# Attention with high and low parts: the low part of the probabilities times 65 columns of v in place of 129

## The chip, the cores and the metric

The kernel runs on one core of one Trainium2 chip. The metric is the device time of one execution in microseconds (us), the median of the runs shown. The engines are TensorE (PE in the rows, its weight loads PEld), VectorE (DVE), ScalarE (ACT), GpSimd (POOL) and the queue that issues the DMAs (SP).

## The reference

A block of a transformer on 4 sequences of 1024 tokens of width 128: attention with 16 heads of 64, then a feed-forward part of width 352 with values rounded to four-bit floats in blocks of 16. What the change touches is the attention:

```python
q = split_heads(x @ Wq.T)
k = split_heads(x @ Wk.T)
v = split_heads(x @ Wv.T)
sim = jnp.einsum('bhid,bhjd->bhij', q, k) * scale
attn = safe_softmax(sim)      # exp(s - max) / (sum + 1e-10)
out = jnp.einsum('bhij,bhjd->bhid', attn, v)
```

All of it is float32. The kernel gets near that precision on TensorE with two 16-bit parts of each number: a high part, and what is left of it as a low part.

## The kernel before

**Tiling.** The 64 pairs of sequence and head are taken two heads at a time, in 32 pairs. Rounds 0 to 33 go over them (here numbered from 0; round r computes pair r-1 while it prepares q, k and v of the next and finishes the one before). In rounds 1 to 32 the round has four units k = 0 to 3 (head k // 2, half k % 2 of the 512 queries), and each unit has eight slots s = 0 to 7, one for each block of 128 keys. The order on every engine is the order in which its own function walks rounds, units and slots; nothing reorders it, and semaphores tie the engines together.

**A slot on TensorE** (`round_` of `tensor`, L554 to L637) has, in this order:
- in odd slots `scores(s)`, two matmuls of 64 rows and 512 columns (L586) that give VectorE the scores of a later unit for its maximum;
- the transposed scores of this unit, two matmuls of 512 columns into `st` (L605, L607). They wait until the exponential of two slots before is taken (`s_ex`);
- the products of the unit before with v (L633), eight matmuls, one per key block j. The stationary operand is a 128x128 block of probabilities, the moving operand a row of `v`. In slots 0, 1, 4 and 5 the probabilities are the high part (the upper 16 bits of `probs`, read as bf16), in slots 2, 3, 6 and 7 the low part `p_low`, called **low slots** below. They add up in `ob[0]` (slots 0 to 3) or `ob[1]` (slots 4 to 7);
- jobs of the table `JOBS`, in odd slots: the projections q, k, v, the transposes, the output projection, parts of the feed-forward.

**v.** A row of `v` for a key block and a head holds, as f16, 64 columns of the high part of v, 64 of the low part and one column of ones, which gives the sum of the probabilities; one more element is not used. `VC = 2 * DH + 1` is 129, and both kinds of slot multiply by all 129 columns.

**The other engines.** ScalarE takes the exponential of each slot (L759, 128x512), reads the sums (`sums`, L727), scales the outputs (`scaled`, L773) and takes the high parts of the projections. GpSimd makes `p_low` of each slot (L449) as soon as its exponential is there, and adds the high and low outputs (`join`, L456). A unit's low parts are needed by TensorE in slot 2 of the next unit. VectorE takes the maxima (L939, one reduction of 1024 columns per odd slot; the next `scores` waits for it, since `sm` has one pair of banks), the low parts of the projections, and the rounding steps of the feed-forward (`quant`, L1085 to L1117), which are placed by hand at certain slots.

## Time and profile before

| | |
|---|---|
| median of 3 runs | 1526.01 us (1524.71 to 1526.96) |
| profiled execution, first to last instruction | 1523.5 us |
| PE busy | 1464.8 us, 96% |
| PE weight loads busy | 973.2 us, 64% |
| POOL busy | 1251.3 us, 82% |
| ACT busy | 1164.4 us, 76% |
| DVE busy | 1081.7 us, 71% |
| L633 with `probs`, 4096 matmuls of 129 columns | 317.3 us busy, 219 ns each from start to end |
| L633 with `p_low`, 4096 matmuls of 129 columns | 316.6 us busy, 219 ns each |

A matmul's 219 ns reach from its start to its end; the next one starts long before that end, so the distance of two starts, and not the mean, says what one takes on the engine. Rounds 1 to 8 have no feed-forward; the rounding of its weights stands in rounds 5, 7 and 8. From round 9 on, rounds come in turns of two (odd and even), with the feed-forward of two tiles of tokens spread over them.

### The profile page before, as it was taken

The page shows a single profiled execution, that of the slowest core. Times are in us where ns is not written, and L with a number is a line of the kernel's source. Part 1 is how long each engine was busy: PE and PEld are TensorE (multiplying, and loading weights), DVE is VectorE, ACT ScalarE, POOL GpSimd, SP SyncE. Part 2 cuts the span into 40 slices and gives each one's busy share as a digit, 9 for nine tenths or more (in the row PEclk, how much of TensorE's full clock was granted, in tenths as well). Part 3 has the DMA queues.
Part 4 walks back from the last instruction along what each step waited for, and adds up shares of the span by engine and source line. Part 5 has one row for each costly group of instructions (what it writes and reads, how often), then busy time and mean ns, then how long its engine had stood idle before and what let it go on. Part 6 is the DMA issues. An engine that isn't in the chain of part 4 may idle for free.

```text
span 1523.5 us, 35256 instructions
## 1 busy us (share of the span) xinstructions
PE 1464.8 (96%) x13828; PEld 973.2 (64%) x13828; DVE 1081.7 (71%) x1717; ACT 1164.4 (76%) x2413; POOL 1251.3 (82%) x1391
## 2 busy tenths in 40 slices
PE   4999999999999999999999999999999999999965
PEld 2566666666666666666666666666666666666644
DVE  7666676677677777676776767677776777767467
ACT  3788888877888878787787878788787878778832
POOL 5888989878888888798888879888888888888932
PEclk8999999999999999999999999999999999999977
DMA  6111111111111111111110111111011110111000
GB/s 168 43 43 43 43 40 26 32 33 43 43 43 43 26 29 40 43 43 47 37 32 22 47 43 42 47 32 37 23 46 43 43 47 23 38 31 47 2 4 14
DMA packets 46660, 59.77 MB, mean 39 GB/s; under 512 B 8672, under 2 KB 21920, under 8 KB 46496
## 3 DMA queue, kind: packets, MB, share of 16 engines
q1 hardware_dynamic: 46336, 57.26, 16.0%
q8 instruction: 111, 1.82, 0.5%
q14 instruction: 53, 0.43, 0.1%
q10 hardware_dynamic: 160, 0.26, 0.0%
HBM read 4.80 MB, written 2.10 MB: 5 GB/s over the span
## 4 chain that ended last, share of the span: by engine, by line
PE 91%; DVE 6%; POOL 1%; ACT 1%; DMA 1%; issue 1%; SPq 0%; DVEq 0%
PE ob L633 29%; PE st L605 17%; PE st L607 14%; PE sm L586 11%; PE mb L522 5%; PE mb L538 4%; PE mb L527 3%; PE mb L1240 2%; PE mb L533 2%; POOL p_low L449 1%; DVE negm L939 1%; PE mb L1251 1%; PE mb L551 1%; PE mb L1246 1%; DMA probs<-wq 0%
## 5 line engine op out<-in xcount | busy, mean ns | idle before, releaser
L449 POOL TENSOR_TENSOR p_low<-probs 128x512 f16<-128x512 f32 x1024 | 1087.4, 1074 | 208.5 <-ACT probs L759 201.7
L759 ACT ACTIVATE probs<-st,lift,exp_scale 128x512 f32<-128x512 f32 x1024 | 793.3, 775 | 189.4 <-PE st L607 169.4
L939 DVE TENSOR_REDUCE negm<-sm 128x1 f32<-128x1024 f32 x508 | 618.1, 1217 | 148.5 <-PE sm L586 148.5
L605 PE MATMUL st<-q_hl,k_hh 128*128 128x512 f16 x1024 | 394.0, 385 | 2.3 <-DMA q_hm<-m_low 2.3
L607 PE MATMUL st<-q_hm,k_l 128*128 128x512 f16 x1024 | 388.7, 380 | 0.0
L633 PEld LDWEIGHTS ob<-v,p_low 128*128 128x128 f16 x4096 | 275.1, 97 | 123.0 <-POOL p_low L449 3.3
L633 PEld LDWEIGHTS ob<-v,probs 128*128 128x128 bf16 x4096 | 276.0, 98 | 120.7 <-ACT probs L759 0.5
L633 PE MATMUL ob<-v,p_low 128*128 128x129 f16 x4096 | 316.6, 219 | 2.5 <-POOL p_low L449 2.4
L633 PE MATMUL ob<-v,probs 128*128 128x129 f16 x4096 | 317.3, 219 | 0.2
L586 PE MATMUL sm<-k_hh,q_hl 64*128 64x512 f16 x508 | 197.5, 389 | 5.7 <-DVE negm L939 5.3
L586 PE MATMUL sm<-k_hh,q_hm 64*128 64x512 f16 x508 | 197.5, 389 | 0.0
L605 PEld LDWEIGHTS st<-q_hl,k_hh 128*128 128x128 f16 x1024 | 99.1, 97 | 134.0 <-issue 116.4
L773 ACT ACTIVATE oscl<-ob,rden 128x128 f32<-128x128 f32 x512 | 157.7, 363 | 1.8 <-DVE rden L928 1.8
L456 POOL TENSOR_TENSOR o_n<-oscl 128x128 f32<-128x128 f32 x256 | 120.3, 470 | 5.4 <-ACT oscl L773 5.4
L607 PEld LDWEIGHTS st<-q_hm,k_l 128*128 128x128 f16 x1024 | 100.5, 98 | 16.3 <-issue 2.8
L907 DVE TENSOR_TENSOR v<-mb,v 128x512 f16<-128x512 f32 x64 | 44.2, 691 | 69.9 <-ACT v L696 69.9
L586 PEld LDWEIGHTS sm<-k_hh,q_hl 64*128 64x128 f16 x508 | 47.0, 93 | 62.7 <-DVE negm L939 6.5
L922 DVE TENSOR_TENSOR x<-x,mb 128x512 f32<-128x512 f32 x64 | 44.0, 687 | 54.9 <-PE mb L538 54.9
L896 DVE SCALAR_TENSOR_TENSOR k_low<-mb,k_scale,k_high 128x512 f16<-128x512 f32 x64 | 47.9, 750 | 49.2 <-ACT k_high L689 49.2
L890 DVE TENSOR_TENSOR q_low<-mb,q_high 128x512 f16<-128x512 f32 x64 | 44.2, 691 | 41.3 <-ACT q_high L682 41.3
L538 PE MATMUL mb<-wo_s,oT 128*128 128x128 f32 x512 | 70.5, 281 | 0.8 <-ACT oT L693 0.8
L696 ACT ACTIVATE v<-mb 128x512 f16<-128x512 f32 x64 | 38.2, 597 | 40.9 <-PE mb L527 40.7
(175 smaller groups left out, 1535.1 us busy)
## 6 DMA issues: line engine op xcount, KB each, us to landing
k_hh<-k_high SPq DMA_DIRECT2D x128, 128.0 KB, 2.3
k_l<-k_low SPq DMA_DIRECT2D x64, 128.0 KB, 2.4
q_hl<-q_high SPq DMA_DIRECT2D x64, 128.0 KB, 2.3
q_hl<-q_low SPq DMA_DIRECT2D x64, 128.0 KB, 2.4
q_hm<-q_high SPq DMA_DIRECT2D x62, 128.0 KB, 2.3
x<-x SPq DMA_DIRECT2D x4, 512.0 KB, 7.2
q_hm<-m_high SPq DMA_DIRECT2D x128, 1.0 KB
q_hm<-m_low SPq DMA_DIRECT2D x128, 1.0 KB
```

The lines of the kernel that those rows point to most:

```text
L449: return pool.tensor_tensor(p_low[b][:, j, :], p, p.bitcast(BF16)[:, 1::2], ALU.subtract)
L456: pool.tensor_tensor(o_n[pq][:, t:t + 2, head * DH:(head + 1) * DH], o[:, :, 0:DH], o[:, :, DH:2 * DH], ALU.add).then_inc(s_on, 1)
L522: last = pe.matmul(bank[:, :], of_pair(wT[w], "qk".index(name[0]), g), of_batch(xT[a], g, c * HALF, HALF), start=(w == 0 and a == 0), stop ...
L538: last = pe.matmul(bank[:, t * P:(t + 1) * P], oT[:, (4 * c + t) * P:(4 * c + t + 1) * P], wo_s[:, bass.ds((g - 2) % PAIRS, 1), :].rearran ...
L586: last = pe.matmul(banks[:, h, :], q_rows[rows, t * P:(t + 1) * P], k_hh[n][rows, h * 512:(h + 1) * 512], start=True, stop=True)
L605: pe.matmul(st[s % 2][:, :], k_hh[n][:, s * P:(s + 1) * P], q_hl[n][:, half * HALF:(half + 1) * HALF], start=True, stop=False)
L607: pe.matmul(st[s % 2][:, :], k_l1[n][:, s * P:(s + 1) * P], q_hm[n][:, half * HALF:(half + 1) * HALF], start=False, stop=True).then_inc(s_ ...
L633: last = pe.matmul(ob[bank][:, o:o + VC], p, v[pq][:, j, ph, 0:VC], start=(j == 0 and s % 4 == 0), stop=(j == JT - 1 and low == 1), skip_g ...
L759: nc.scalar.activation(probs[k % 2][:, s, :], st[s % 2][:, :], ACT.Exp, bias=lift[:, 0:1], scale=exp_scale[:, head, pair:pair + 1]).then_i ...
L773: last = nc.scalar.activation(oscl[bank][:, t, :], ob[bank][:, t * OT:t * OT + 2 * DH], ACT.Copy, scale=rden[:, bank, t:t + 1])
L896: nc.vector.scalar_tensor_tensor(out=k_parts[1][:, cols], in0=bank[:, :], scalar=k_scale[:, g % PAIRS:g % PAIRS + 1], in1=k_parts[0][:, cols],
L939: nc.vector.tensor_reduce(negm[k % 2][:, s // 2:s // 2 + 1], banks[:, :, :].rearrange("p a n -> p (a n)"), AX.X, ALU.max, negate=True).the ...
```

## The change

The row of `v` is stored as one, high, low, starting at element 1 of its 130: the ones column at 1, the high part at 2 to 65, the low part at 66 to 129. `VC` stays 129. The high part of the probabilities still meets all 129 columns. The low part meets the first `VL = 65`, the ones and the high part of v. The product of the two low parts is left out. The reads of `ob` move with it (the sum is in column 0 of each half, the outputs behind it). The instructions of every engine, their order and their waits are the same as before; half of the L633 matmuls have 65 moving columns where they had 129.

```diff
-VC = 2 * DH + 1
+VC = 1 + 2 * DH
+VL = 1 + DH
...
                                 o = (t % 2) * OT
-                                last = pe.matmul(ob[bank][:, o:o + VC], p, v[pq][:, j, ph, 0:VC],
+                                n = VL if low else VC
+                                last = pe.matmul(ob[bank][:, o:o + n], p, v[pq][:, j, ph, 1:1 + n],
                                                  start=(j == 0 and s % 4 == 0), stop=(j == JT - 1 and low == 1),
                                                  skip_group_check=True)
...
-                    nc.scalar.activation(v[1 - q][:, 4 * c:4 * c + 4, :, 0:DH],
+                    nc.scalar.activation(v[1 - q][:, 4 * c:4 * c + 4, :, 2:2 + DH],
                                          bank[:, :].rearrange("p (t h d) -> p t h d", t=4, h=2), ACT.Copy).then_inc(s_vh, 1)
...
-                nc.scalar.activation(den[:, bank, :], ob[bank][:, 2 * DH:2 * DH + OT + 1:OT], ACT.Copy, bias=EPS_LIFTED
+                nc.scalar.activation(den[:, bank, :], ob[bank][:, 0:OT + 1:OT], ACT.Copy, bias=EPS_LIFTED
                                      ).then_inc(s_dn, 1)
...
-                    last = nc.scalar.activation(oscl[bank][:, t, :], ob[bank][:, t * OT:t * OT + 2 * DH], ACT.Copy,
+                    last = nc.scalar.activation(oscl[bank][:, t, :], ob[bank][:, t * OT + 1:t * OT + VC], ACT.Copy,
                                                 scale=rden[:, bank, t:t + 1])
...
-                nc.vector.memset(v[n][:, :, :, 2 * DH:VC], 1.0).then_inc(s_init, 1)
+                nc.vector.memset(v[n][:, :, :, 1:2], 1.0).then_inc(s_init, 1)
...
-                    nc.vector.tensor_tensor(part[:, :, :, DH:2 * DH], bank[:, :].rearrange("p (t h d) -> p t h d", t=4, h=2),
-                                            part[:, :, :, 0:DH], ALU.subtract).then_inc(s_v, 1)
+                    nc.vector.tensor_tensor(part[:, :, :, 2 + DH:2 + 2 * DH], bank[:, :].rearrange("p (t h d) -> p t h d", t=4, h=2),
+                                            part[:, :, :, 2:2 + DH], ALU.subtract).then_inc(s_v, 1)
```

## Rows read from the trace of the kernel before

**Rows 1.** The page, parts 1 and 2: busy time of engines, TensorE's granted clock.
```profile
PE 1464.8 (96%) x13828; PEld 973.2 (64%) x13828; DVE 1081.7 (71%) x1717; ACT 1164.4 (76%) x2413; POOL 1251.3 (82%) x1391
...
PEclk8999999999999999999999999999999999999977
```

**Rows 2.** The page, part 4: the chain that ended last, by engine and by line.
```profile
PE 91%; DVE 6%; POOL 1%; ACT 1%; DMA 1%; issue 1%; SPq 0%; DVEq 0%
PE ob L633 29%; PE st L605 17%; PE st L607 14%; PE sm L586 11%; PE mb L522 5%; PE mb L538 4%; PE mb L527 3%; PE mb L1240 2%; PE mb L533 2%; POOL p_low L449 1%; DVE negm L939 1%; PE mb L1251 1%; PE mb L551 1%; PE mb L1246 1%; DMA probs<-wq 0%
```

**Rows 3.** The page, part 5: groups; busy us, mean ns | idle before, releaser.
```profile
L449 POOL TENSOR_TENSOR p_low<-probs 128x512 f16<-128x512 f32 x1024 | 1087.4, 1074 | 208.5 <-ACT probs L759 201.7
L759 ACT ACTIVATE probs<-st,lift,exp_scale 128x512 f32<-128x512 f32 x1024 | 793.3, 775 | 189.4 <-PE st L607 169.4
...
L633 PEld LDWEIGHTS ob<-v,p_low 128*128 128x128 f16 x4096 | 275.1, 97 | 123.0 <-POOL p_low L449 3.3
...
L633 PE MATMUL ob<-v,p_low 128*128 128x129 f16 x4096 | 316.6, 219 | 2.5 <-POOL p_low L449 2.4
L633 PE MATMUL ob<-v,probs 128*128 128x129 f16 x4096 | 317.3, 219 | 0.2
```

**Rows 4.** Timeline of PE, unit 3 of round 21: start us, us, group.
```profile
962.31 0.38 PE L605 MATMUL st<-q_hl,k_hh 128*128 128x512 f16 x1
...
962.74 0.62 PE L633 MATMUL ob<-v,p_low 128*128 128x129 f16 x8
963.29 0.39 PE L586 MATMUL sm<-k_hh,q_hl 64*128 64x512 f16 x1
...
963.61 0.39 PE L605 MATMUL st<-q_hl,k_hh 128*128 128x512 f16 x1
...
964.05 0.62 PE L633 MATMUL ob<-v,p_low 128*128 128x129 f16 x8
964.51 0.38 PE L605 MATMUL st<-q_hl,k_hh 128*128 128x512 f16 x1
```

**Rows 5.** Timeline of the weight loads (PEld) at the same place.
```profile
965.81 0.10 PEld L605 LDWEIGHTS st<-q_hl,k_hh 128*128 128x128 f16 x1 [0.23 <-issue]
965.83 0.10 PEld L607 LDWEIGHTS st<-q_hm,k_l 128*128 128x128 f16 x1
```

**Rows 6.** Timeline of PE: scores that wait for VectorE, end of round 22.
```profile
1006.20 0.39 PE L586 MATMUL sm<-k_hh,q_hl 64*128 64x512 f16 x1
...
1013.58 0.39 PE L586 MATMUL sm<-k_hh,q_hl 64*128 64x512 f16 x1
```

**Rows 7.** Timeline of DVE over the same stretch, nothing but work between.
```profile
1006.64 1.22 DVE L939 TENSOR_REDUCE negm<-sm 128x1 f32<-128x1024 f32 x1 [0.54 <-PE sm L586]
...
1012.14 1.21 DVE L939 TENSOR_REDUCE negm<-sm 128x1 f32<-128x1024 f32 x1
```

**Rows 8.** The same two views in slots 3 and 4 of unit 3, round 21.
```profile
959.64 1.21 DVE L939 TENSOR_REDUCE negm<-sm 128x1 f32<-128x1024 f32 x1
...
961.09 0.39 PE L586 MATMUL sm<-k_hh,q_hl 64*128 64x512 f16 x1
```

**Rows 9.** Timeline of POOL, unit 3 of round 21 and on; of PE, its next user.
```profile
957.13 1.04 POOL L449 TENSOR_TENSOR p_low<-probs 128x512 f16<-128x512 f32 x1 [1.76 <-ACT probs L759]
...
960.99 4.33 POOL L449 TENSOR_TENSOR p_low<-probs 128x512 f16<-128x512 f32 x4
...
965.88 3.03 POOL L449 TENSOR_TENSOR p_low<-probs 128x512 f16<-128x512 f32 x3
...
967.90 0.62 PE L633 MATMUL ob<-v,p_low 128*128 128x129 f16 x8
```

**Rows 10.** Stretches: us, then busy us of each engine; rounds 21, 4 and 5.
```profile
920.14:964.51 44.37, 44.37 (x437) 29.96 (x435) 34.84 (x57) 36.11 (x77) 39.45 (x45) 1.00 0.17 40
...
163.54:206.76 43.22, 43.22 (x427) 28.80 (x425) 27.41 (x39) 37.51 (x79) 38.48 (x42) 1.00 0.16 38
206.76:251.72 44.96, 42.86 (x423) 28.30 (x421) 33.89 (x62) 34.61 (x71) 38.81 (x45) 1.00 0.16 37
```

## Prediction

> **What bounds the kernel now.** I read the page's busy times first [rows 1]: PE is at work for 1464.8 of 1523.5 us, at a granted clock of nine tenths or more but for the first and the last slices, so at its upper level (2.4 GHz) nearly throughout. The chain that ended last says the same of the path: PE has 91% of it, and line L633, the products with v, 29%, the largest share of one line [rows 2]. The groups show the other side: L633 waited 2.5 us (low part) and 0.2 us (high part) in all, while ScalarE's exponentials waited 189.4 us, mostly for TensorE, and GpSimd's `p_low` 208.5 us for those exponentials [rows 3]. So TensorE sets the pace, and the others follow it with idle time.
>
> What one L633 matmul takes is read from the distance of starts, in the timeline [rows 4]: the run of eight that begins at 964.05 is followed by L605 at 964.51, so 0.46 us for eight, 57 ns each. The page's 219 ns are from start to end and overlap. The check: 29% of 1523.5 us is 442 us, over 8192 matmuls 54 ns.
>
> **What the change takes from TensorE.** Only the 4096 matmuls with `p_low` change, from 129 to 65 moving columns. The two levels needed are a price per column and a fixed price. In [rows 4] the two matmuls of 512 columns from 962.31 to 962.74 take 0.43 us, 215 ns each; against 57 ns for 129 columns that is 158 ns over 383 columns, 0.41 ns a column, the 2.4 GHz level. 64 columns fewer are 64 x 0.41 = 26.4 ns, which leaves about 30 ns for a matmul of 65 columns. I take 26.5 ns: 4096 x 26.5 = 108.5 us, 0.21 us in each of the 512 low slots.
>
> No row has 16-bit matmuls shorter than 128 columns in a row, so whether the weight load of 128x128 before each fits under 30 ns is bounded from two sides. Upper end of the pace: the loads follow the matmuls at 57 ns, and the trace would look the same if a load took up all of that; then nothing is gained. Lower end: the loads of L605 and L607 start at 965.81 and 965.83, 10 to 20 ns apart, both of 128x128 in 16 bits [rows 5], which puts the time for which a load holds its path at 20 ns or less; the 97 ns of its row [rows 3] are from start to end. I take the lower end, since these rows are the same operation: 20 ns fit under 30.
>
> The TensorE page of the Trainium skill (TensorE: Matmul & The Clock Gate, section LDWEIGHTS) speaks against this change: it prices a load by its columns, 107 ns for 128, and the section on fast weight load measures about half of that for 16-bit data, some 53 ns. By the second figure the load would set the pace at 65 columns and the gain would be some 4 ns a matmul, 16 us in all. The loads 10 to 20 ns apart speak against it here.
>
> Nothing else costs a thing by itself. The copies, the subtraction and the memset keep their sizes; the reads of `ob` start one column further or at the front. The moving operand starts at an odd 16-bit element where it started at an even one; no row shows that case. From 0 to an unknown price; I take 0 since the stationary operand `probs` is already read at odd elements with a stride of two and L633 moves at the same pace with it (busy 317.3 against 316.6 us for the contiguous `p_low` [rows 3]). The odd start comes back as a rival.
>
> **What takes some of it back.** A shorter slot is a gain only while the others are there in time. I went along each place where TensorE waits for another engine, took the time left before, and subtracted 0.213 us for each low slot that lies inside.
>
> *ScalarE.* A slot's exponential starts when its second matmul has ended and takes 775 ns [rows 3]: for the slot that starts at 962.31 that is about 962.90 to 963.70, and the slot that needs the bank starts at 964.51 [rows 4]. 0.8 us are left; two low slots lie between, so 0.4 us remain. No loss.
>
> *VectorE, feed-forward rounds.* VectorE has work without a gap from the reduction at 1006.64 to the end of the one at 1012.14, 1013.35 [rows 7]; it starts 0.44 us after its scores at 1006.20, and the scores that need its end start at 1013.58 [rows 6]. 0.23 us are left, less some 0.05 us for the signal. Three low slots lie between (slots 6 and 7 of unit 3, slot 2 of unit 0): 3 x 0.213 = 0.64, so TensorE will wait 0.64 - 0.18 = 0.46 us. It comes in 11 of the 12 double rounds: 5.1 us. In unit 3 of the odd rounds a second such chain ends at 960.85, the scores start at 961.09 [rows 8], and two low slots lie inside: 0.43 - 0.19 = 0.24 us, 12 times, 2.9 us. Together 8 us.
>
> *VectorE, rounding of the weights.* Round 5 is 44.96 us long with PE busy 42.86 [rows 10]: one unit of it already waits for VectorE. There, and in rounds 7 and 8, four low slots gain nothing: 0 to 3 x 0.86 us, I take 2.
>
> *GpSimd.* In unit 3 of round 21 it starts at 957.13 and the unit's last low part ends about 965.88 + 1.01 = 966.89; TensorE uses it at 967.90 [rows 9]. 1.0 us is left, four low slots lie between, 0.15 us remains. So it comes out even there. In the attention-only rounds it has less: round 4 takes 43.22 us with POOL busy 38.48 [rows 10], and would take 43.22 - 16 x 0.213 = 39.8. After rounds 3, 5 and 7 the bias of a sequence is added on GpSimd as well. Between 0 and 2 us for each of the eight rounds; I take 1.5 for two of them, 3 us in all. Behind the last unit TensorE already waits 2.4 us for `p_low` [rows 3], and the low slots ahead of it only make that longer: 1 us.
>
> The sum: 108.5 - 8 - 2 - 3 - 1 = 94.5 us. The profiled execution would go from 1523.5 to 1429 us; the median of the runs was 2.5 us above the profiled span, so 1431.5 us for the runs, 6.2% less.
>
> **The rivals.**
>
> *The weight load sets the pace.* The load is as large for 65 columns as for 129. If it holds its path for 50 ns or more, a low slot stays as it is, and the time is between 1510 and 1526 us. For it: the pace of 57 ns says nothing against it, and all rows of 16-bit runs show 57. Against it: [rows 5].
>
> *Something between.* The issue of load and matmul, two instructions in 30 ns, or the turn-round of adding to the same columns of `ob` twice as often, may hold the pace between 33 and 50 ns. At 40 ns the gain is 4096 x 17 = 70 us, less of it is taken back (the chains of VectorE have more room), some 8: 1464 us. The same TensorE page (section Wait — 56ns, not 53.3ns?) states a floor of about 25 ns between starts however few the columns, and about 62 ns a matmul if the sequencer's code issues each; the 57 ns of [rows 4] do not hold with the second, and the first would not bind.
>
> *GpSimd becomes the bound.* It is busy 39.45 us in round 21 [rows 10], with 32 low parts of 1.074 us [rows 3], against 44.37 - 3.4 + 0.7 = 41.7 us for TensorE. It decides once a low part takes 0.07 us more. At 1.2 us a round would take 39.45 + 32 x 0.126 = 43.5 us, 1.8 more than forecast, and the time would be some 1480 us. Against it: [rows 9] show four in 4.33 us, 1.08 each, with VectorE at work beside them.
>
> *The odd start of v slows every product.* This is the rival on the other side. All 8192 matmuls now read v from an odd 16-bit element. If TensorE reads its moving operand in pairs of elements and splits a pair that is cut, a matmul would stream at up to half its pace: 129 columns at 2 x 54 = 108 ns, 65 columns at 54. That is +51 ns for 4096 and -3 for the others, some 195 us: 1720 us. Smaller prices decide from 108.5 / 8192 = 13 ns a matmul on. For it there is nothing but the absence of a row; against it, the stationary operand at odd elements costs nothing.
>
> **How the numbers follow.** The forecast, with its waits, 0.78; a pace between 0.10; the load sets the pace 0.05; GpSimd 0.04; the odd start 0.03. The predicted time is the forecast's, 1431.5 us. Without any wait it would be 1526.0 - 108.5 = 1417.5, with waits twice those I count 1446; a pace of 40 ns gives 1464. To leave out no more than 2 in 10 the range goes from 1420 to 1464. 0.2% is 3 us, about what a measurement of this kernel can tell. Faster by more than that: 0.78 + 0.10 + 0.04, and 0.02 of the load's 0.05, for a load that ends a little short of 57 ns: 0.94. Within 0.2%: the other 0.03 of the load's. Slower: 0.03.
>
> **What would show it.** In the timeline after, eight L633 matmuls with `p_low` should take 0.24 us from first start to the next group's start, eight with `probs` still 0.46: the first tells the load's rival and the pace between, the second the odd start. PE's waits for VectorE's `negm` should rise by 8 to 10 us, and appear at slot 1 and slot 3 of unit 0 and slot 5 of unit 3. The wait for `p_low` should be below 8 us; above 20, GpSimd is the bound. A wait of L605 for the exponentials would be a miss of mine. Busy times of ScalarE, VectorE and GpSimd should not change by more than 1%. The forecast is wrong if an odd round such as 21, 44.37 us before [rows 10], does not take between 41 and 42.5.

## The result, and the profile after

| | before | after |
|---|---|---|
| median of 4 runs | 1526.49 us (1524.71 to 1528.37) | 1464.06 us (1463.79 to 1465.67) |
| profiled execution, first to last instruction | 1523.5 us | 1462.2 us |
| ratio, with its 95% interval | | 0.9595 (0.9583 to 0.9606) |

The change takes 62 us. The forecast was 94.5 us: 1431.5 us, with a range that ended at 1464.0. The time is 32.6 us above the forecast, and just outside the range.

The page of the changed kernel, its busy times, granted clock, the chain and the groups that answer to [rows 1 to 3]:

```profile
PE 1380.1 (94%) x13828; PEld 892.1 (61%) x13828; DVE 1101.9 (75%) x1717; ACT 1137.5 (78%) x2413; POOL 1245.4 (85%) x1391
...
PEclk8999999999999999999999999999999999999958
...
PE 65%; DVE 20%; POOL 6%; ACT 5%; issue 3%; DMA 1%; SPq 0%; DVEq 0%
...
L450 POOL TENSOR_TENSOR p_low<-probs 128x512 f16<-128x512 f32 x1024 | 1083.0, 1076 | 148.2 <-ACT probs L761 145.1
...
L587 PE MATMUL sm<-k_hh,q_hl 64*128 64x512 f16 x508 | 197.5, 389 | 23.1 <-DVE negm L941 23.0
L635 PE MATMUL ob<-v,p_low 128*128 128x65 f16 x4096 | 211.2, 195 | 5.4 <-POOL p_low L450 5.3
```

Three things stand in them. TensorE is busy 85 us less. On the chain that ended last, TensorE had 91% and VectorE 6% [rows 2]; now they have 65% and 20%. And VectorE, whose instructions are the same 1717, is busy 20 us *more*: 1101.9 against 1081.7 us [rows 1]. The waits of TensorE for VectorE's maxima rose from 5.3 to 23.0 us:

```profile
PE sm L587 <- DVE negm L941: 23.0, 55, 4.6
```

(total, times, longest). The forecast had them rise by 8 to 10.

Did the step on which the sum stood happen? TensorE's timeline in unit 3 of round 21, the place of [rows 4]:

```profile
923.42 0.38 PE L606 MATMUL st<-q_hl,k_hh 128*128 128x512 f16 x1
...
923.85 0.41 PE L635 MATMUL ob<-v,p_low 128*128 128x65 f16 x8
924.20 0.39 PE L587 MATMUL sm<-k_hh,q_hl 64*128 64x512 f16 x1
...
924.52 0.39 PE L606 MATMUL st<-q_hl,k_hh 128*128 128x512 f16 x1
...
924.96 0.41 PE L635 MATMUL ob<-v,p_low 128*128 128x65 f16 x8
925.21 0.38 PE L606 MATMUL st<-q_hl,k_hh 128*128 128x512 f16 x1
```

Eight low matmuls that begin at 924.96 are followed by L606 at 925.21: 0.25 us where it was 0.46, so 31 ns each and not 57. The slot from 923.42 to 924.52 took 1.10 us; before, 962.31 to 963.61, it took 1.30 [rows 4]. Wherever TensorE waits for nothing a low slot is 0.207 us shorter (forecast 0.212). Over 512 low slots these are 106.0 us. The span fell by 61.3 us. So 44.7 us were given back, where the forecast had 14; 2.8 of them are the 5.5 ns by which each of the 512 other slots became longer. I compared the two traces slot by slot, from the starts of the matmuls of L605 and L606, and took what each slot lost against 0.207 us for each low slot:

| where | given back, us | forecast |
|---|---|---|
| odd rounds 11 to 31: 11 x 2.05 | 22.5 | 8 |
| even rounds 10 to 30: 11 x 0.28 | 3.1 | 0 |
| rounds 5, 7, 8 (rounding of weights): 2.1, 1.05, 7.3 | 10.4 | 2 |
| rounds 1, 2, 3, 4, 6, 9 | 5.3 | 3 |
| round 32, the start, the tail: 1.4, 0.6, 1.2 | 3.2 | 1 |

The largest single one is in round 8. The timelines of VectorE, GpSimd and TensorE there, and TensorE's stretches (length, then busy time and count of PE, PEld, DVE, ACT, POOL, then the granted clock, DMA share, GB/s):

```profile
337.05 0.51 DVE L1087 TENSOR_REDUCE q_small<-wd 128x22 f32<-128x352 f32 x1
337.60 5.27 DVE L1089 TENSOR_SCALAR q_small<-q_small 128x22 f32<-128x22 f32 x1
342.90 0.18 DVE L1093 TENSOR_SCALAR q_small<-q_small 128x22 f32<-128x22 f32 x1
```

```profile
334.38 4.04 POOL L450 TENSOR_TENSOR p_low<-probs 128x512 f16<-128x512 f32 x4
338.38 0.47 POOL L457 TENSOR_TENSOR o_n<-oscl 128x128 f32<-128x128 f32 x1
338.79 4.05 POOL L450 TENSOR_TENSOR p_low<-probs 128x512 f16<-128x512 f32 x4
345.91 0.45 POOL L457 TENSOR_TENSOR o_n<-oscl 128x128 f32<-128x128 f32 x1 [3.08 <-ACT oscl L775]
```

```profile
345.15 0.61 PE L587 MATMUL sm<-k_hh,q_hl 64*128 64x512 f16 x1 [4.61 <-DVE negm L941]
```

```profile
342.00:344.00 2.00, 0.00 (x0) 0.00 (x0) 1.90 (x5) 0.00 (x0) 0.83 (x1) 0.81 0.00 0
344.00:346.00 2.00, 0.84 (x3) 0.24 (x4) 2.00 (x5) 0.63 (x2) 0.09 (x1) 0.50 0.00 0
346.00:348.00 2.00, 2.00 (x15) 1.63 (x14) 1.07 (x1) 0.78 (x1) 0.74 (x2) 0.50 0.06 17
348.00:350.00 2.00, 2.00 (x10) 1.39 (x10) 0.93 (x2) 0.08 (x1) 0.67 (x1) 0.50 0.87 200
350.00:352.00 2.00, 2.00 (x23) 1.43 (x22) 1.16 (x3) 1.76 (x4) 1.04 (x1) 0.98 0.79 181
```

A VectorE step of 22 columns, which took 0.23 us in the same place before, took 5.27 us. It ends at 342.87, and GpSimd's run of low parts that stands back to back since before 334.38 ends at 338.79 + 4.05 = 342.84. The maxima stand behind that step in VectorE's queue, TensorE waits 4.61 us for them. Its granted clock, 1.00 up to 343, falls to 0.50, the 1.2 GHz level (0.81 is the mean of the two microseconds in which it falls), and is back near 1.00 after 350. Round 8 loses 7.3 us by a wait of 4.6.

The same thing in small is in every feed-forward round. Groups of VectorE with the shapes kept apart, of before:

```profile
L1117 DVE TENSOR_TENSOR hidden<-qv,q_small 128x704 f32<-128x704 f32 x12 | 10.4, 869 | 0.0
...
L1113 DVE SCALAR_TENSOR_TENSOR qv<-qw,qv 128x256 f32<-128x256 f32 x12 | 8.8, 734 | 0.0
```

and the same two lines of after:

```profile
L1119 DVE TENSOR_TENSOR hidden<-qv,q_small 128x704 f32<-128x704 f32 x12 | 17.5, 1462 | 0.0
...
L1115 DVE SCALAR_TENSOR_TENSOR qv<-qw,qv 128x256 f32<-128x256 f32 x12 | 13.5, 1122 | 0.0
```

The same instruction on the same data took 869 ns and takes 1462; another 734 and 1122. The reductions of the maxima did not change: 1216 ns. The steps that grew read and write SBUF alone, the reductions read the scores from PSUM. Not every step between SBUF tensors grew: the product of the scales with `hidden` (704 columns) takes 1205 ns before and 1207 after. GpSimd is busy as long as before, in a shorter span, so 85% of the time where it was 82%.

What happens at `hidden` is seen where it meets GpSimd, in slot 6 of unit 1 of round 21. Before:

```profile
940.36 1.78 POOL L449 TENSOR_TENSOR p_low<-probs 128x512 f16<-128x512 f32 x1 [0.21 <-ACT probs L759]
940.37 0.87 DVE L1117 TENSOR_TENSOR hidden<-qv,q_small 128x704 f32<-128x704 f32 x1
```

and after:

```profile
902.10 1.04 POOL L450 TENSOR_TENSOR p_low<-probs 128x512 f16<-128x512 f32 x1
902.37 1.52 DVE L1119 TENSOR_TENSOR hidden<-qv,q_small 128x704 f32<-128x704 f32 x1
```

Before, GpSimd had paused for 0.21 us and the two start within 0.01 us of each other: GpSimd's instruction takes 1.78 us in place of 1.04 and `hidden` takes 0.87. After, that pause is gone and GpSimd is 0.27 us into its instruction: now `hidden` waits for its end at 903.14 and then takes 0.74. So at this place the wait went from GpSimd to VectorE, by who is there first. The means hide it: 11 of the 12 take 1.52 us, the last, behind the last low part, 0.86.

### The profile page after: what moved, and what is told of

It is laid out like the page before. It is cut to its first block, busy times and chain, and to the rows that moved or that the text cites. A ratio compares the mean times of both kernels' runs of the same rounds, so it can differ in the third digit from the quotient of the medians.

```text
span 1462.2 us, 35256 instructions
## 1 busy us (share of the span) xinstructions
PE 1380.1 (94%) x13828; PEld 892.1 (61%) x13828; DVE 1101.9 (75%) x1717; ACT 1137.5 (78%) x2413; POOL 1245.4 (85%) x1391
## 4 chain that ended last, share of the span: by engine, by line
PE 65%; DVE 20%; POOL 6%; ACT 5%; issue 3%; DMA 1%; SPq 0%; DVEq 0%
PE ob L635 16%; PE st L606 12%; PE st L608 10%; PE sm L587 8%; DVE negm L941 7%; POOL p_low L450 5%; PE mb L523 4%; PE mb L539 4%; PE mb L528 2%; PE mb L1242 2%; PE mb L534 2%; ACT probs L761 1%; DVE v L909 1%; DVE qv L1115 1%; DVE hidden L1119 1%
## 5 line engine op out<-in xcount | busy, mean ns | idle before, releaser
L450 POOL TENSOR_TENSOR p_low<-probs 128x512 f16<-128x512 f32 x1024 | 1083.0, 1076 | 148.2 <-ACT probs L761 145.1
L941 DVE TENSOR_REDUCE negm<-sm 128x1 f32<-128x1024 f32 x508 | 617.6, 1216 | 105.4 <-PE sm L587 104.2
L606 PE MATMUL st<-q_hl,k_hh 128*128 128x512 f16 x1024 | 394.7, 385 | 2.3 <-DMA q_hm<-m_low 2.3
L635 PEld LDWEIGHTS ob<-v,probs 128*128 128x128 bf16 x4096 | 279.3, 98 | 123.1 <-ACT oscl L775 1.0
L635 PE MATMUL ob<-v,probs 128*128 128x129 f16 x4096 | 322.4, 222 | 0.6 <-ACT oscl L775 0.5
L635 PEld LDWEIGHTS ob<-v,p_low 128*128 128x128 f16 x4096 | 195.7, 98 | 127.7 <-POOL p_low L450 8.7
L635 PE MATMUL ob<-v,p_low 128*128 128x65 f16 x4096 | 211.2, 195 | 5.4 <-POOL p_low L450 5.3
L606 PEld LDWEIGHTS st<-q_hl,k_hh 128*128 128x128 f16 x1024 | 99.3, 97 | 134.5 <-issue 108.7
L539 PEld LDWEIGHTS mb<-wo_s,oT 128*128 128x128 f32 x512 | 65.7, 198 | 3.7 <-ACT oT L695 1.1
```

What stands on the lines that cost most here:

```text
L450: return pool.tensor_tensor(p_low[b][:, j, :], p, p.bitcast(BF16)[:, 1::2], ALU.subtract)
L539: last = pe.matmul(bank[:, t * P:(t + 1) * P], oT[:, (4 * c + t) * P:(4 * c + t + 1) * P], wo_s[:, bass.ds((g - 2) % PAIRS, 1), :].rearran ...
L606: pe.matmul(st[s % 2][:, :], k_hh[n][:, s * P:(s + 1) * P], q_hl[n][:, half * HALF:(half + 1) * HALF], start=True, stop=False)
L635: last = pe.matmul(ob[bank][:, o:o + n], p, v[pq][:, j, ph, 1:1 + n], start=(j == 0 and s % 4 == 0), stop=(j == JT - 1 and low == 1), skip ...
L941: nc.vector.tensor_reduce(negm[k % 2][:, s // 2:s // 2 + 1], banks[:, :, :].rearrange("p a n -> p (a n)"), AX.X, ALU.max, negate=True).the ...
```

## The theories

**Mine:** the pace of the low matmuls is what the forecast said. What it missed is that VectorE's steps between SBUF tensors can wait while GpSimd works. A shorter slot takes pauses from GpSimd and no work; so more of those steps find it at work and grow, and with them VectorE's chain, on which TensorE now waits.

**Rivals:** (a) the odd start of v costs something in all 8192 product matmuls, and the loss is spread; (b) the weight load holds the pace above what 65 columns need; (c) GpSimd is the bound directly, by `p_low` arriving late; (d) it is the order of the jobs on ScalarE and VectorE and not how long anything takes.

## Experiments on the pace of TensorE

**v from an even element.** The row of v as low, high, one from element 0; the low part meets elements 64 to 128, again 65 columns.

```diff
-VC = 1 + 2 * DH
-VL = 1 + DH
+VC = 2 * DH + 1
+VL = DH
...
-                                n = VL if low else VC
-                                last = pe.matmul(ob[bank][:, o:o + n], p, v[pq][:, j, ph, 1:1 + n],
+                                n = VL if low else 0
+                                last = pe.matmul(ob[bank][:, o + n:o + VC], p, v[pq][:, j, ph, n:VC],
```

> The row of v is stored as low, high, one from element 0, so that the low part of the probabilities meets elements 64 to 128, again 65 columns, but from an even start; all else as in the changed kernel. Port theory (the gain is held back because VectorE's steps between two SBUF tensors wait while GpSimd works on its low parts, which it does with fewer gaps once TensorE's slots are short): the start is worth at most 4 ns in a group of eight, so 1461 to 1465 us. Rival, the odd start slows TensorE's products and is why the forecast was missed: 1435 us or less. Both expect eight low matmuls in 0.25 us.

Measured: 1462.16 us (1461.66 to 1462.89), ratio to before 0.958 (0.9566 to 0.9594). 1.9 us below after, nearly all of the 33 are still there.

**The new layout with 129 columns for both.** The other half of the change alone.

```diff
-                                n = VL if low else VC
+                                n = VC
```

> The changed layout (one, high, low from element 1) with 129 columns for both parts, as before. Port theory: 1526 to 1530 us, within 0.3% of the kernel before. Rival, the odd start costs the missing 30 us: 1550 us or more.

Measured: 1530.21 us (10 runs, 1528.47 to 1531.43), ratio 1.0024 (1.0015 to 1.0034). The odd start costs 3.7 us; in the timeline it is 5 ns in a group of eight matmuls. Rival (a) of the theories is true with a price of 0.6 ns a matmul; the prediction's rival needed 13 to decide.

**97 columns, and 33.** The low part meets the ones and the high part and half of the low part of v (97); or the ones and half of the high part (33: the other half of the high part is left out for the low probabilities).

```diff
-VL = 1 + DH
+VL = 1 + DH + DH // 2
```

> The changed kernel with 97 columns for the low part (ones, high v and half of low v): TensorE's slots shorten by half as much, 53 us in all. Port theory: the gaps of GpSimd close only gradually, so the gain is nearer to the full 53 than at 65 columns: 1526 - 53 + 2 (odd start) + 8 to 14 = 1483 to 1490 us. Rival, a fixed loss that comes with any shortening: 1500 us or more.

```diff
-VL = 1 + DH
+VL = 1 + DH // 2
```

> The changed kernel with 33 columns for the low part (ones and half of high v, so half of the product of low probabilities and high v is left out). If the matmul's width still set its pace, the low slots would fall by another 13 ns a matmul, 54 us in all, to a pace of 16 ns. Port theory: the weight load (10 to 20 ns) and GpSimd's work bound it, less than half of the 54 us is seen: 1440 to 1455 us. Rival, TensorE is still the only bound: 1410 us.

Measured: 97 columns 1492.57 us (1488.64 to 1494.09; the profiled one spanned 1486.7), ratio 0.978 (0.9763 to 0.9797), a little above the range that I had expected; 33 columns 1455.18 us (1454.69 to 1457.65), ratio 0.9542 (0.9528 to 0.9556), just above its range. The pace of a low matmul by its columns: 129 columns 55 to 60 ns, 97 columns 42 to 47, 65 columns 29 to 35, 33 columns 25 to 28 (means 57, 44, 31 and 26). From TensorE's timeline with 33 columns:

```profile
919.15 0.36 PE L635 MATMUL ob<-v,p_low 128*128 128x33 f16 x8
919.37 0.38 PE L606 MATMUL st<-q_hl,k_hh 128*128 128x512 f16 x1
```

From 129 to 97 to 65 columns the pace falls by 13 ns each time, 0.41 ns a column, as worked out in the prediction. The next 32 columns take only some 5 ns: no pace below 25 ns was seen, and 65 columns stand just above it. Had the width still set the pace, it would have been 16 ns; a slot gained 0.04 us and not 0.1. The Trainium skill (TensorE: Matmul & The Clock Gate, section Wait — 56ns, not 53.3ns?) states a floor of about 25 ns between starts; the 33 columns agree with it. Its price for the fast load of 16-bit weights, some 53 ns, does not hold as a pace here: each of these matmuls has its own load of 128x128, at 31 and at 25 ns. Rival (b) has fallen.

With 97 columns half of the gain in each slot (0.100 us) gives 51.2 us before any wait, and the span of the profiled execution fell by 36.8: 14.4 given back, where 65 columns give back 44.7. That execution was the fastest of the four; by the medians it is 17.3. The odd rounds say it more clearly: with half of the gain they lose 0.5 us each, with all of it 2.05. There the loss grows faster than the gain. That is how a margin on another engine looks that is used up, and not how a price on TensorE looks.

## Experiments on GpSimd and VectorE

**Half of the low part, after and before.** GpSimd subtracts 256 of the 512 columns of each block. The low part of the other 256 is left out (it stays zero), so half of the correction is missing; TensorE's work is the same.

```diff
+            for n in range(2):
+                pool.memset(p_low[n][:, :, HALF // 2:HALF], 0.0)
...
-                return pool.tensor_tensor(p_low[b][:, j, :], p, p.bitcast(BF16)[:, 1::2], ALU.subtract)
+                return pool.tensor_tensor(p_low[b][:, j, 0:HALF // 2], p[:, 0:HALF // 2], p.bitcast(BF16)[:, 1:HALF:2], ALU.subtract)
```

> The changed kernel, but GpSimd subtracts only the first 256 of 512 columns of each slot's low part; the others stay zero from the start. So half of the low part of the probabilities is left out. TensorE does all its matmuls. Port theory: GpSimd's L450 takes some 0.55 us in place of 1.08, has gaps after each, VectorE's L1119 on the hidden values goes from 1.46 back to about 0.87 us, the 5.3 us step of round 8 to about 0.25 us, and the time falls from 1464 to 1430 to 1442 us. Rival, VectorE's own chains of work are too long whatever GpSimd does: VectorE's means stay, and the time is 1455 to 1464 us.

The same edit in the kernel before, as a control:

> The same halving of GpSimd's low part in the kernel before (half of the low part of the probabilities left out). It is the control: there TensorE sets the pace nearly throughout, so both theories expect little, 1518 to 1526 us.

Measured: after with half 1430.85 us (1429.43 to 1431.95), ratio 0.9377 (0.9361 to 0.9392): 33.2 us less than after. Before with half 1515.77 us (1515.40 to 1517.68), ratio 0.9933 (0.9918 to 0.9948): 10.6 us less than before, more than either theory expected. So the half of GpSimd's work costs 22.6 us more in the changed kernel than in the old one. That is the larger part of the 32.6 that were missing. (By the profiled executions it is 34.7 less 7.8; the start and the tail have 3.4 us of that difference, the rounds the rest.) The page of after with half, and the two VectorE groups again:

```profile
PE 1367.4 (96%) x13828; PEld 885.5 (62%) x13828; DVE 1052.4 (74%) x1717; ACT 1131.6 (79%) x2413; POOL 829.8 (58%) x1393
...
L1121 DVE TENSOR_TENSOR hidden<-qv,q_small 128x704 f32<-128x704 f32 x12 | 10.4, 868 | 0.0
...
L1117 DVE SCALAR_TENSOR_TENSOR qv<-qw,qv 128x256 f32<-128x256 f32 x12 | 5.3, 445 | 0.0
```

With nothing changed on VectorE it is busy 1052.4 us, 49.5 less than after. In the old kernel the same step took 32.4 us from it (1081.7 to 1049.3). So 17 of the 20 us by which VectorE's time grew are new waits behind GpSimd. `hidden` is back at 868 ns; the 256-column step, 734 before, is at 445, so it had waited already in the kernel before. TensorE's wait for the maxima falls to 8.0 us. Round by round, the losses in (unit 0, slot 0), (0,2), (1,7) and (3,4) of the odd rounds are gone, and of 7.3 us in round 8 nothing is left; 0.27 us at (0,7) and 0.37 at (2,6) stay.

**As busy, half of it only writing.** That run takes GpSimd's lateness away together with what it does to VectorE. So a memset of 448 columns of scratch goes ahead of each half subtraction: GpSimd is busy as long as after, but reads SBUF in only 0.64 of 1.1 us. The same half of the low part is left out.

```diff
+                wait(pool, s_fl, len(filled) - 1)
+                pool.memset(filler[:, len(filled) % 2, :], 0.0).then_inc(s_fl, 1)
+                filled.append(j)
                 return pool.tensor_tensor(p_low[b][:, j, 0:HALF // 2], p[:, 0:HALF // 2], p.bitcast(BF16)[:, 1:HALF:2], ALU.subtract)
```

> As the run that halves GpSimd's low part (half of the low part of the probabilities left out), but ahead of each half subtraction GpSimd fills a scratch tile of 448 f16 columns, which reads nothing from SBUF. So GpSimd is as busy as in the changed kernel, about 1.1 us a slot, and only half of that time is a read. Port theory in its narrow form (VectorE's steps wait for GpSimd's reads): 1430 to 1442 us, VectorE's L1119 and L1115 on the hidden values near 0.9 us. Rival, what matters is how late GpSimd is with the low parts, the sums and the roots, or any GpSimd instruction holds VectorE: 1455 us or more.

Measured: 1452.59 us (1451.04 to 1453.19), ratio 0.9519 (0.9503 to 0.9535): between the two, 11.5 us below after and 21.7 above the half alone. Its groups on GpSimd and VectorE:

```profile
L458 POOL TENSOR_TENSOR p_low<-probs 128x256 f16<-128x256 f32 x1024 | 651.2, 636 | 0.0
...
L456 POOL MEMSET filler<- 128x448 f16 x1024 | 482.4, 471 | 156.9 <-ACT probs L769 152.1
...
L1127 DVE TENSOR_TENSOR hidden<-qv,q_small 128x704 f32<-128x704 f32 x12 | 10.4, 865 | 0.0
...
L1097 DVE TENSOR_SCALAR q_small<-q_small 128x22 f32<-128x22 f32 x1 | 5.0, 4995 | 0.0
```

The two kinds of step part here. `hidden`, with two inputs in SBUF, is back at 865 ns though GpSimd is as busy as ever. A step at another place, L1123 with 704 columns (L1115 of after), was not freed, 1126 ns for 1171; it may have met the reading half. The step of 22 columns with one input waits 5.0 us all the same, and other steps with one input grew beyond what they took after: L1110, 704 columns, 872 ns for 578, and L1097, 44 columns, 867 for 530. GpSimd's memsets and VectorE's steps have no data in common. So the wait is not one for data, and what counts depends on the kind of both instructions. The Trainium skill (SBUF — State Buffer, section Who interferes with whom) says this: VectorE and GpSimd share a pair of ports, an exclusive lock, that a VectorE operation needs in a two-port mode, or with two inputs in SBUF against a GpSimd operation that reads. After, the half and this run agree with it for both kinds. It also says that the one that starts first keeps the pair for its instruction. `hidden` in round 21 agrees, before and after; but in round 8 the wait lasted 5.27 us, over the rest of one low part, a join and four more low parts, none of which is longer than 1.1 us. There the measurement goes further than the page.

Neither expectation was met: the narrow form of the theory, in which only GpSimd's reads hold VectorE, asked for 1442 us or less, its rival for 1455 or more. Of the 33.2 us, 11.5 come back when half of GpSimd's time no longer reads (some 2 of them in the start and the tail). They are a net figure, since the writes made other steps longer. The other 21.7 come with GpSimd being busy, by its writes, which hold the steps with one input, or by its own lateness. The runs do not part these two.

**The low part in two instructions of 256 columns.** If a step waits for one instruction of GpSimd, shorter instructions would shorten the wait.

```diff
-                return pool.tensor_tensor(p_low[b][:, j, :], p, p.bitcast(BF16)[:, 1::2], ALU.subtract)
+                for h in range(2):
+                    at = slice(h * HALF // 2, (h + 1) * HALF // 2)
+                    last = pool.tensor_tensor(p_low[b][:, j, at], p[:, at], p.bitcast(BF16)[:, 1 + h * HALF:(h + 1) * HALF:2],
+                                              ALU.subtract)
+                return last
```

> The changed kernel with each of GpSimd's low parts made by two instructions of 256 columns in place of one of 512. Port theory: a step of VectorE that waits for the instruction in flight waits half as long, so L1119 on the hidden values falls from 1.46 to about 1.1 us; but each half costs GpSimd about 0.1 us more (642 ns each in the run with half of the work, against 1076 for the whole), so its gaps close and the steps that wait for a gap wait longer: 1464 to 1490 us. If VectorE were served at each end of an instruction, round 8's 22-column step would fall from 5.3 us to below 1 us. Rival, the size of GpSimd's instruction does not matter and GpSimd is not what holds VectorE: 1464 us and no mean moved.

Measured: 1574.26 us (1573.22 to 1576.18), ratio 1.0319 (1.0303 to 1.0334). Far beyond both expectations, and slower than the kernel before. Two halves take 628 ns each, 1.26 us a block for 1.076. From its page and waits:

```profile
PE 1409.8 (90%) x13828; PEld 901.7 (57%) x13828; DVE 1154.1 (73%) x1717; ACT 1141.8 (73%) x2413; POOL 1389.2 (88%) x2415
...
PE ob L639 <- POOL p_low L452: 26.9, 25, 3.9
```

```profile
L1093 DVE TENSOR_SCALAR q_small<-q_small 128x22 f32<-128x22 f32 x1 | 7.7, 7679 | 0.0
```

TensorE now waits 26.9 us for `p_low` itself, but 71.3 us for VectorE's maxima, where after had 23.0:

```profile
PE sm L591 <- DVE negm L945: 71.3, 55, 5.5
```

The chain that ended last runs through `p_low` for 35% of the span, where it did for 5% after. Two things are in this time. The first is the prediction's rival, GpSimd as the bound. It was to decide from 0.07 us more per block on; here it got 0.18. In round 4 GpSimd is busy for all of its 43.05 us (38.9 of 40.8 after), in round 21 for 43.8 of 44.25. The prediction's sum gives 39.45 + 32 x 0.182 = 45.3 us for round 21, so it is about right there. But rounds 4 and 21 took only 2.3 and 1.1 us more than after. The second thing is in the even rounds 12 to 30, for which the same sum gives 36.7 + 5.8 = 42.5 us, hardly more than the 42.1 of after. Round 22 takes 48.4, with GpSimd busy for 41.2. These ten rounds hold 65 of the 112 us. In each of them one VectorE step of 256 columns waits:

```profile
L1123 DVE TENSOR_TENSOR xn<-qv,q_small 128x256 f32<-128x256 f32 x12 | 69.8, 5815 | 0.0
```

```profile
1001.12 6.17 DVE L1123 TENSOR_TENSOR xn<-qv,q_small 128x256 f32<-128x256 f32 x1
```

The same group took 710 ns after. GpSimd worked on its low parts and a join without a pause until 1007.00, and the step ended at 1007.29. It is the thing of round 8 once more, now in ten even rounds: with nothing changed on VectorE the kernel lost more where VectorE waited than where GpSimd set the pace.

And the length of GpSimd's instruction? `hidden` fell from 1462 to 1200 ns, near the 1.1 us that I had expected. In round 21 it waited from 965.79 to the end of the half in flight at 966.27 and then took 0.75; GpSimd's next half, which stood ready, took 1.25 us for 0.63. So for `hidden` the wait is one for the end of an instruction. For the steps of 22 columns (7.7 us, with instructions half as long) and of 256 columns it is not.

**Slot 7's low part on VectorE.** One eighth of the low parts, made at the start of the next unit.

```diff
-                            low_part(k % 2, s).then_inc(s_lp, 1)
+                            if s < SLOTS - 1:
+                                low_part(k % 2, s).then_inc(s_lp, 1)
...
+                        if s == 0 and (prev if k == 0 else cur):
+                            wait(dve, s_ex, 8 * unit)
+                            p = probs[1 - k % 2][:, SLOTS - 1, :]
+                            nc.vector.tensor_tensor(p_low[1 - k % 2][:, SLOTS - 1, :], p, p.bitcast(BF16)[:, 1::2],
+                                                    ALU.subtract).then_inc(s_l7, 1)
```

> The changed kernel, but the low part of slot 7 of each unit is made by VectorE at the start of the next unit, so GpSimd makes seven of eight. Nothing is left out. Port theory: GpSimd's unit falls from about 9.6 to 8.6 us and has gaps again, VectorE's has 0.7 us more, where its chains have room in the even rounds; the 22-column step of round 8 falls below 3 us, the waits for p_low vanish: 1445 to 1462 us. Rival, VectorE's total work is the bound: 1470 us or more.

Measured: 1483.28 us (1480.94 to 1486.89), ratio 0.9723 (0.9705 to 0.9741), 19 us above after: the rival was right. The page has

```profile
PE 1385.2 (93%) x13828; PEld 894.0 (60%) x13828; DVE 1201.1 (81%) x1845; ACT 1139.4 (77%) x2413; POOL 1123.5 (76%) x1263
```

122 us off GpSimd, 99 us onto VectorE, and `hidden` still takes 1461 ns. So GpSimd's share of busy time, lower here than before the change, does not by itself say how long a step waits; where the two meet does. The step of 22 columns fell to 0.9 us, as the theory had it. It is VectorE's chain that TensorE waits for, and work put there comes out on TensorE, however much room GpSimd has.

## Experiments on the order

**The third rounding of the weights one round later.** This moves the 22-column step of round 8 to another neighbourhood.

```diff
-W_QUANT = ((5, AT_W), (7, AT_W2), (8, AT_W))
+W_QUANT = ((5, AT_W), (7, AT_W2), (9, AT_W))
```

> The changed kernel with the rounding of w_down moved from round 8 to round 9, same slots. Round 8 follows a bias that GpSimd adds at the end of round 7, so GpSimd works without a gap there, and a VectorE step of 22 columns took 5.3 us. Port theory: in round 9 GpSimd has gaps, that step takes at most 1 us, and the time falls by 5 to 8 us, to 1456 to 1459. Rival, the step is slow by itself or VectorE's total work counts: no change, 1462 to 1465.

Measured: 1458.35 us (1456.24 to 1460.17), ratio 0.9559 (0.9545 to 0.9574). The step takes 0.92 us in round 9. Round 8 loses nothing any more, round 9 loses 3.4 us more, at (1,2) and (1,7), where VectorE now has both tasks: some 6 us net.

**The same, with job `o1` ahead of `h0` in slot (1,7).** `h0` waits for VectorE's `hidden`, the step that grew from 869 to 1462 ns; `o1` doesn't.

```diff
-("g0", 0, (1, 7), (2, 0), (2, 2)), ("h0", 0, (1, 7), (2, 0), None),
-        ("w2", 0, (1, 7), (2, 0), None), ("o1", 1, (1, 7), None, (2, 0)),
+("g0", 0, (1, 7), (2, 0), (2, 2)), ("o1", 1, (1, 7), None, (2, 0)),
+        ("h0", 0, (1, 7), (2, 0), None), ("w2", 0, (1, 7), (2, 0), None),
```

> The changed kernel with the rounding of w_down in round 9 (as run before, 6 us) and the job o1 ahead of h0 in slot 7 of unit 1, so that TensorE has other work while VectorE's last rounding step of the hidden values waits for GpSimd. In the changed kernel TensorE loses 0.38 us there in each of 11 rounds. Port theory: that wait is covered, 4 us, to 1452 to 1456. Rival, TensorE only meets the next late step: 1458.

Measured: 1452.75 us (1452.23 to 1453.90), ratio 0.9523 (0.9507 to 0.9539), 5.6 below the run before it. The loss at (1,7) falls from 0.38 to 0.08 us in each odd round, 3.4 us in all. Another 0.9 us are saved at the same slot in round 9, and the tail, which the edit does not touch, is 2 us shorter than in the run before; round 7, which it does not touch either, is 1.5 us longer.

**Two of ScalarE's steps two slots later.** At (0,7) and (2,6) the loss had stayed with GpSimd halved. ScalarE's timeline after, slot 5 of unit 0 of round 21, shows what stands there:

```profile
890.29 0.79 ACT L1127 ACTIVATE qw<-qw 128x704 f32<-128x704 f32 x1 [0.52 <-DVE qw L1102]
890.99 0.76 ACT L761 ACTIVATE probs<-st,lift,exp_scale 128x512 f32<-128x512 f32 x1
```

The exponential of that slot waits behind a step of the feed-forward that waits for VectorE. At (2,6) it is the normalisation (L1228), which waits for GpSimd's root.

```diff
-AT_ROOT, AT_STATS, AT_NORM = (2, 0), (2, 0), (2, 3)
+AT_ROOT, AT_STATS, AT_NORM = (2, 0), (2, 0), (2, 5)
...
-AT_X_LIFT, AT_H_LIFT = (3, 5), (0, 5)
+AT_X_LIFT, AT_H_LIFT = (3, 5), (0, 7)
```

> The changed kernel with two pieces of ScalarE's work for the feed-forward placed later: the rounding step of the hidden values (L1127) from slot 5 of unit 0 to slot 7, the normalisation of two tiles (L1228) from slot 3 of unit 2 to slot 5. Theory of ScalarE's order: in the changed kernel these pieces wait for VectorE and GpSimd ahead of an exponential and make the one in that slot 0.5 to 0.9 us late; the losses of 0.27 us in slot 7 of unit 0 and of 0.37 us in slot 6 of unit 2 go, in 11 odd rounds: 7 us, to about 1457 us. Rival, these two places too belong to GpSimd or VectorE: 1462 to 1465 us, or the loss turns up one or two slots later.

Measured: 1462.56 us (1460.63 to 1463.00), ratio 0.9582 (0.9568 to 0.9596), 1.5 us below after and in the rival's range. Both losses are gone, 0.64 us a round, as I had them. But 0.31 us appear at (1,0), where nothing had been lost. Of 2.05 us an odd round still loses 1.72: a part of the wait turned up two slots later. Round 7 loses 1.6 us more than after, as it did in the run with the jobs swapped, so that is not this edit's doing.

**All of it together.** The even start, the rounding in round 9, the swapped jobs and ScalarE's two steps, in one kernel with 65 columns.

> All that helped together: v stored as low, high, one (even start), the rounding of w_down in round 9, o1 ahead of h0, and the two pieces of ScalarE's work later. If the causes are separate, the gains add: 1464 - 2 - 11.5 - 7 = 1443.5 us, 1441 to 1447. Rival, they hide one another: 1449 to 1453 us.

Measured: 1444.99 us (1444.44 to 1445.12), ratio to before 0.9468 (0.9452 to 0.9484). This is the fastest kernel that computes all that the changed one does, 19 us under after. The four gains apart were 1.9, 11.3 (the rounding and the jobs) and 1.5 us, 14.7 in all; together they are 19.1. Slot by slot they come from the odd rounds (11 losses of 1.34 us for 2.05: 7.8), the even ones (1.5), rounds 1 to 9 (5.1) and from the start and the tail (4.5). The last is of no edit's doing: start and tail together differ by up to 7 us among the kernels of this case, from 4.4 us less than before to 2.6 more. So it is not shown that the edits help each other. TensorE still waits 17.2 us for the maxima.

## Why the prediction was wrong

**The bound and the pace: right.** TensorE set the pace, the load of the weights fits under 30 ns, 64 columns fewer are worth 26 ns. 106.0 us were gained for 108.5 forecast. The rival by the load, and the one between (40 ns a matmul), did not come, although that one's time of 1464 is what was measured: it was the right number by the wrong way, since there was no pace of 40 ns in the trace.

**The odd start: right in size.** It was taken as 0 and is 3.7 us with 129 columns.

**VectorE in the feed-forward rounds: right where the durations stayed, too small where they grew.** The chain of 0.24 us at (3,4) came out at 0.23. The chain of 0.46 us came out at 0.65 (0.38 at (0,0) and 0.27 at (0,2)). The third, 0.38 us at (1,7), wasn't in the sum: before, `hidden` was in time there, and it was late once it took 0.59 us more. These three are 1.26 us in each of 11 rounds, 13.9 us for the 8 forecast.

**ScalarE, "No loss": wrong.** I took the time that is left to an exponential from TensorE's slots alone. The losses of 0.27 and 0.37 us at (0,7) and (2,6), 7.0 us in all, come from steps of the feed-forward that stand ahead of the exponential in ScalarE's order and wait for VectorE and GpSimd. The run with these two moved away shows the place, though not the price: it won only 1.5 us, since 3.4 of the 7.0 came back at (1,0). The rows for it were in the trace of before.

**The rounding of the weights, "I take 2": 10.4 us.** 7.3 of it is the one step of 22 columns. The bound that I gave, 3 x 0.86, was what TensorE could fail to gain; it could not hold a step that becomes 20 times as long, nor the granted clock of 0.50 that follows it.

**GpSimd: about right where I looked, wrong in what it reaches.** TensorE's waits for `p_low` are 5.3 us, for 2.4 before and the bound of 8 that the text set; rounds 1 to 4, 6 and 9 lose 5.3 us for the 3 forecast. A low part takes 1076 ns for 1074, so the rival that GpSimd becomes the bound did not come by its own mechanism. The run with the low part in two instructions shows that with 0.18 us more per block it does bind, in rounds 4 and 21; the 0.07 at which I put the point were not tried.

**The step that failed** is in "What takes some of it back", and one sentence carries it: "Busy times of ScalarE, VectorE and GpSimd should not change by more than 1%". I went along VectorE's chains with the durations of before. VectorE's time grew by 1.9%, and all of that growth lies in steps between SBUF tensors: `hidden` 7 us, the two steps `qv<-qw,qv` of 256 columns 7 us, the steps of 22 columns 4 us, and the rest in steps of the same kind. (ScalarE's busy time fell by 2.3%, but its instructions did not become shorter, 779 ns for 775: more of their records overlap. GpSimd's stayed within 0.5%.) The control says how much hangs on GpSimd: 22.6 us. ScalarE's order is another 7.0, the smaller gain per slot 2.5. They make 32.1 of the 32.6 us, but that they come so near is in part luck: the halved subtraction also takes away losses that the forecast had, and the 7.0 are read from the slots and were not won back by a run. For the odd rounds the text asked for 41 to 42.5 us in round 21; it took 43.11:

```profile
882.10:925.21 43.11, 41.94 (x441) 27.46 (x437) 36.14 (x58) 35.58 (x77) 39.29 (x45) 1.00 0.17 41
925.21:967.30 42.09, 42.09 (x432) 26.96 (x429) 30.30 (x44) 34.08 (x72) 36.49 (x42) 1.00 0.17 40
```

and VectorE, busy 34.84 us in it before [rows 10], is busy 36.14. Round 22, without such steps, lost 0.3 us.

That VectorE's durations hang on GpSimd could have been read from the trace of before. Its groups on VectorE, the shapes kept apart:

```profile
L1095 DVE TENSOR_TENSOR qv<-xn,q_small 128x256 f32<-128x256 f32 x12 | 12.1, 1006 | 0.4
...
L1095 DVE TENSOR_TENSOR probs<-probs,wd 128x704 f32<-128x704 f32 x4 | 3.6, 891 | 0.1
```

The same operation of one line takes 1006 ns for 256 columns in the rounds, beside GpSimd's low parts, and 891 ns for 704 columns in the tail, where GpSimd works little. With half of GpSimd's work the first takes 586 ns. A time that does not follow the size says that the instruction waits inside itself, and such waits can grow when the pauses of the other engine shrink.

**What stays open.** Why the step in round 8 waited for the whole of GpSimd's run. The timelines of GpSimd and VectorE of before at the same rounding show the next step of 22 columns (the one of 5.27 us had been through in 0.23 us just ahead of it):

```profile
353.13 3.33 POOL L449 TENSOR_TENSOR p_low<-probs 128x512 f16<-128x512 f32 x3
...
353.26 0.96 DVE L1091 TENSOR_SCALAR q_small<-q_small 128x22 f32<-128x22 f32 x1
```

This step was through at 354.22, about where the first of three low parts ends, and did not wait for the other two. What differs by the trace is how far GpSimd was behind: there its second low part began 0.14 us after its exponential had ended, in round 8 the low parts began 0.6 to 1.7 us after theirs. That GpSimd gives no turn while the next instruction stands ready would fit these rows, but not as a general rule: with the low part in two instructions `hidden` got its turn between two halves that both stood ready, in the same kernel in which the step of 256 columns waited through ten. And of the 21.7 us that come with a busy GpSimd that half the time only writes, the part of its writes and the part of its lateness were not told apart.

## What to carry to other kernels

Taking time from the engine that bounds takes pauses from all others: an engine whose instructions collide with another's may then need more time for the same instructions, as VectorE did here by 20 us, so a forecast of its waits must not use the durations of before as constants. Look ahead of the change for instructions of one operation whose times do not follow their size, ask with whom they collide, and see in the timeline which of the two is there first. And go along the order of *each* engine at the places where it waits for a third, since a chain with 0.4 us to spare by the slots may have none by what stands ahead in its queue.

## What the runs showed of the hardware that was not expected

- A VectorE step of 22 columns between SBUF tensors waited 5.27 us (7.68 us with the low part in two instructions, 0.23 us before) behind GpSimd instructions of 1.0 us each. With half of GpSimd's time spent on writes alone, a step with one input still waited 5.0 us, and `hidden`, with two inputs, took 865 ns where it had taken 1462. Reductions from PSUM took 1215 to 1218 ns in every kernel.
- A VectorE step of 256 columns between SBUF tensors took 6.17 us in the even rounds from 12 on with the low part in two instructions, 0.71 us after: the longest wait was not set by the length of GpSimd's instructions.
- Where `hidden` and a low part met in round 21, the one that started second waited for the other: GpSimd's instruction took 1.78 us for 1.04 before, VectorE's 1.52 for 0.87 after.
- A wait of TensorE of 4.6 us was followed by a granted clock of 0.50 for the next 6 us from 344 to 350, and the slots from the wait on lost 7.1 us, the wait among them.
- Pairs of a 128x128 load and a matmul in 16 bits run at 55 to 60 ns with 129 columns, 42 to 47 with 97, 29 to 35 with 65, 25 to 28 with 33: 0.41 ns a column down to 65 columns, and none below 25 ns.
- The moving operand from an odd 16-bit element costs 5 ns in eight matmuls of 129 columns.
